# A selective scan in 1024-wide pieces: two scans a unit, with the carries added to the input, and the product with C shared anew between two engines

## The chip, the cores and the metric

One core of one Trainium2 chip. The metric is device time in microseconds (us) for one execution. Engines by their short names: PE is TensorE, DVE is VectorE, ACT is ScalarE, POOL is GpSimd, SP is SyncE. Every instruction stream is in order, and every dependency between engines is a semaphore written out by hand.

## The reference, cut to what matters

A Mamba block and then a mixture of experts, all in float32, on 8 sequences of 1024 tokens with 256 channels. The change is in the selective scan:

```
dA = exp(dt_t[:, :, None] * A[None])
dBu = (dt_t * u_t)[:, :, None] * B_t[:, None, :]
h = dA * h + dBu
y = einsum('bdn,bn->bd', h, C_t)
```

It has 512 inner channels, 16 states and 1024 time steps a sequence. `h` starts at zero in each of the 8 sequences. Before it lie a layer norm, an input projection, a convolution of four taps and the projections that give dt, B and C. After it come a gate, an output projection, a second norm, a router that picks 2 of 8 experts, and the expert products on tiles of 128 gathered tokens.

## The kernel before

The 8192 tokens are worked in 16 **blocks** `q` of T = 512 time steps. Two blocks make one sequence: an **even block** starts from a zero state, an **odd block** from the state that the even one left in `carry`. A block has UN = 16 **units** `n` (u = 16q + n). A unit is 128 inner channels (chunk c = n // 4) times 4 states (g = n % 4), laid out as 4 **segments** j. In each segment the 128 partitions hold 4 states of 32 channels, and the 512 time steps lie along the free dimension. Per unit:

- POOL `drive(u)` (L1326) multiplies the whole 128x2048 driving term `hs` = dt*u times B, one unit ahead. `hs` has three buffers, so it waits (through `s_ymm`) until PE has read unit u-3.
- ACT `decay(u, j)` (L977) writes exp(dt*A) of a segment into the PSUM tile `dA`, which has one buffer. Decays of the next unit are written when DVE has used the present one: segments 0 and 1 after the product L1123, segment 2 after L1136, segment 3 after its scan.
- DVE `scan` (L1114) runs one recurrence of 512 steps a segment, in the order 0, 1, 3, 2. It starts from 0.0 or from `carry[:, n, j]`. Segments 0 and 1 are multiplied by C in one 128x1024 product (L1123), segment 2 in a 128x512 product (L1136).
- POOL `weigh(u)` (L1334) multiplies segment 3 by C. The last column is left out in even blocks, since ACT still has to read the state there: `keep01`, `keep2` and `keep3` (L981, L985, L991, L994) copy the last states to `carry`, and `keep3` does that last product itself.
- PE `weigh` (L699) sums the states of a unit into `yps`.

The loops over `s` are **slots**: in slot s each engine works unit s, and between its parts of the unit whatever else is listed for the slot. That other work is the front of the next blocks, in the tables `MAKES` and `TAKES` (PE makes a result in the one PSUM bank `ring`, ACT takes it). It is also `round_off`, `less_lost`, `plus_relu`, `dtu` (four POOL steps of the softplus, by `pieces`), `deviation` (small POOL steps of the norms), `route`, `weights` and `place` (DVE, slots 6 and 8), the scatter of tokens (POOL, slots 8 to 11), and the expert tiles (`tile_transpose`, `gate_up`, `tanh`, `activate`, `down`, `take_y`, `add_rows`). SP issues the loads: `load_rep` brings dt and dt*u of a chunk, repeated for each of 4 states, from DRAM into `rep_dt` and `rep_dtu`, one chunk ahead. After unit 255 only expert tiles of the last block are left.

In DVE's slot, all that matters for the order is:

```
unit_first(s)      # scans 0 and 1, product L1123
unit_third(s)      # scan 3
weights, place     # slot 8 only
unit_second(s)     # scan 2
activate           # two 128x256 steps of an expert tile, in 8 of 16 slots
unit_last(s)       # product L1136
gated, route       # slots 0, 4, 8, 12 and slot 6
```

## Time and profile before

| | |
|---|---|
| median of 3 runs | 2355.94 us (2353.19 to 2358.41) |
| span of the profiled execution | 2343.2 us |
| DVE busy | 1891.2 us (81%) |
| POOL busy | 1961.7 us (84%) |
| ACT busy | 1808.0 us (77%) |
| PE busy, weight loads | 1793.1 us (77%), 922.2 us (39%) |
| mean granted TensorE clock | 0.884 |

The span is from the first to the last instruction of the one execution that was profiled. The profile gives no device time of its own for it, so 12.7 us lie between its span and the median. Times in rows are from the start of the span. From about 600 us to 1900 us the trace repeats with a period of two blocks, about 263 us. The stretch quoted below is one such period: block 8 (even) has its first scan at 1122.73 us, block 9 (odd) at 1255.4 us.

A busy share says how long an engine had an instruction in it. Neighbouring instructions of one engine can overlap in the trace by some 0.1 us, and on POOL by more: where the next one starts before the row's end, the distance between two starts is the better price.

### The profile page before, as it was taken

The numbers are of one execution on the slowest core, as the hardware profiler recorded it, in microseconds if no ns is written. First come the engines' busy times: TensorE is split into PE (matmuls) and PEld (weight loads), VectorE is DVE, ScalarE is ACT, GpSimd is POOL, SyncE is SP. The second block draws the span as 40 slices with busy tenths as digits, with TensorE's granted clock in tenths as the row PEclk, the third lists the DMA queues.
The fourth block names the chain that finished last, engine by engine and source line by source line (L and its number), as shares of the span: only waits on it lengthen the run. The fifth ranks groups of instructions, "written<-read, shape, count | busy, mean of one in ns | idle before, by whom it ended". The sixth has DMA issues, their size and how long they took to land.

```text
span 2343.2 us, 32677 instructions
## 1 busy us (share of the span) xinstructions
PE 1793.1 (77%) x7694; PEld 922.2 (39%) x7694; DVE 1891.2 (81%) x2437; ACT 1808.0 (77%) x3753; POOL 1961.7 (84%) x1320
## 2 busy tenths in 40 slices
PE   5666767597879778797878778697879788675785
PEld 2212323153435344353434344353435344343542
DVE  0399988898989988898979988898989989999221
ACT  5888878888888878888888878888888878763332
POOL 1588897989989898999989898989989898987333
PEclk9788878797989989898989999898989989786998
DMA  1545455477768777677768787677768787797332
GB/s 57 136 90 135 109 134 115 121 170 179 172 159 198 174 192 171 165 184 172 175 158 199 174 197 174 159 176 175 175 157 201 176 193 166 181 259 221 71 51 33
DMA packets 217980, 369.35 MB, mean 158 GB/s; under 512 B 31040, under 2 KB 86592, under 8 KB 217664
## 3 DMA queue, kind: packets, MB, share of 16 engines
q1 hardware_dynamic: 192208, 333.56, 58.0%
q0 software_dynamic: 25584, 33.71, 7.4%
q8 instruction: 65, 1.06, 0.2%
q14 instruction: 123, 1.01, 0.2%
HBM read 285.05 MB, written 83.01 MB: 157 GB/s over the span
## 4 chain that ended last, share of the span: by engine, by line
POOL 31%; issue 25%; PE 14%; ACT 12%; DVE 10%; DMA 7%; POOLq 1%; DVEq 0%; ACTq 0%; SPq 0%
POOL arena L1326 11%; DMA out<-yt,xt 6%; DVE dA L1114 5%; POOL arena L1334 5%; PE ring L605 4%; POOL sorted_x L1364 4%; POOL out L1374 3%; POOL rst L1290 3%; ACT dA L977 2%; DVE arena L1114 2%; POOL arena L1344 2%; POOL arena L1349 2%; PE yps L699 2%; PE ring L613 1%; PE ring L625 1%
## 5 line engine op out<-in xcount | busy, mean ns | idle before, releaser
L1326 POOL TENSOR_TENSOR arena<-arena,b_bc 128x2048 f32<-128x2048 f32 x256 | 998.6, 3901 | 64.8 <-PE yps L699 64.5
L977 ACT ACTIVATE dA<-arena,a_s 128x512 f32<-128x512 f32 x1024 | 680.7, 684 | 120.9 <-DVE arena L1123 74.7
L1114 DVE TENSOR_TENSOR_SCAN dA<-dA,arena 128x512 f32<-128x512 f32 x384 | 454.7, 1214 | 175.2 <-ACT dA L977 108.8
L1114 DVE TENSOR_TENSOR_SCAN dA<-dA,carry,arena 128x512 f32<-128x512 f32 x384 | 477.6, 1275 | 66.6 <-POOL arena L1326 49.8
L699 PE MATMUL yps<-arena,const_s 128*32 128x512 f32 x2048 | 321.3, 704 | 84.1 <-POOL arena L1334 53.6
L1334 POOL TENSOR_TENSOR arena<-arena,c_bc 128x511 f32<-128x511 f32 (+1 forms) x256 | 335.6, 1311 | 28.0 <-DVE arena L1114 26.4
L1123 DVE TENSOR_TENSOR arena<-dA,c_bc 128x1024 f32<-128x1024 f32 x256 | 313.6, 1225 | 8.8
L1374 POOL DMA_INDIRECT out<-yt,xt x135 | 214.7, 1590 | 116.5 <-ACT yt L1018 84.5
L597 PE MATMUL ring<-arena 128*128 128x512 f32 x488 | 271.7, 684 | 52.9 <-ACT arena L881 24.5
L731 PEld LDWEIGHTS p_g<-xT,w_e 128*128 128x128 f32 x1680 | 218.8, 211 | 125.4 <-issue 125.4
L605 PE MATMUL ring<-arena 128*128 128x512 f32 x480 | 235.3, 635 | 33.7 <-ACT arena L881 12.1
L731 PE MATMUL p_g<-xT,w_e 128*128 128x128 f32 x1680 | 238.8, 301 | 21.1 <-issue 12.0
L711 PE MATMUL p_a<-w_e,hT 128*128 128x256 f32 x420 | 128.2, 434 | 110.6 <-ACT xT L1010 81.4
L1136 DVE TENSOR_TENSOR arena<-dA,c_bc 128x512 f32<-128x512 f32 x256 | 176.4, 689 | 5.2
L1114 DVE TENSOR_TENSOR_SCAN arena<-dA,carry,arena 128x512 f32<-128x512 f32 x128 | 163.2, 1275 | 9.4 <-ACT dA L977 9.4
L1114 DVE TENSOR_TENSOR_SCAN arena<-dA,arena 128x512 f32<-128x512 f32 x128 | 155.3, 1213 | 18.4 <-ACT dA L977 18.4
L1364 POOL DMA_INDIRECT sorted_x<-xf,pos x128 | 127.5, 996 | 48.8 <-issue 33.5
L597 PEld LDWEIGHTS ring<-arena 128*128 128x128 f32 x488 | 93.5, 213 | 183.3 <-issue 91.7
L605 PEld LDWEIGHTS ring<-arena 128*128 128x128 f32 x480 | 90.7, 199 | 159.3 <-issue 94.8
L711 PEld LDWEIGHTS p_a<-w_e,hT 128*128 128x128 f32 x420 | 85.8, 215 | 158.7 <-issue 112.9
L699 PEld LDWEIGHTS yps<-arena,const_s 128*32 128x32 f32 x2048 | 43.5, 115 | 252.8 <-issue 166.1
L625 PE MATMUL ring<-w_out_s,sz 128*128 128x256 f32 x512 | 122.7, 382 | 4.5 <-ACT uc L885 3.6
(173 smaller groups left out, 2995.7 us busy)
## 6 DMA issues: line engine op xcount, KB each, us to landing
arena<-dt_d SPq DMA_DIRECT2D x512, 256.0 KB
w_e<-in_w_moe SPq DMA_DIRECT2D x105, 512.0 KB, 4.7
dt_d<-arena SPq DMA_DIRECT2D x128, 256.0 KB, 2.4
w_e<-in_w_moe SPq DMA_DIRECT2D x105, 256.0 KB
xt<-sorted_x SPq DMA_DIRECT2D x135, 129.0 KB
b_bc<-bc_d SPq DMA_DIRECT2D x256, 64.0 KB, 2.4
c_bc<-bc_d SPq DMA_DIRECT2D x256, 64.0 KB, 3.5
xs<-in_x SPq DMA_DIRECT2D x16, 512.0 KB, 4.4
```

The source lines that it names most:

```text
L597: last = pe.matmul(bank(q, name), w_in_s[:, c, ch * P:(ch + 1) * P], xnT[:, c, :], start=c == 0, stop=c == DC - 1)
L605: last = pe.matmul(bank(q, f"W{c}"), d_conv[:, c, k, :], ubuf[:, c % 2, k:k + T], start=k == 0, stop=k == TAPS - 1)
L699: last = pe.matmul(yps[32 * j:32 * j + 32, :], sumsel, hs[:, u % 3, j, :], start=False, stop=g == G - 1, skip_group_check=True)
L711: last = pe.matmul(p_a[:, DM:2 * DM], hT[:, v % 2, c, :], w_e[:, v % 2, col:col + DM], start=c == 0, stop=c == DC - 1)
L731: last = pe.matmul(p_g[:, f, :], w_e[:, v % 2, col:col + P], xT[:, v % 2, c, :], start=c == 0, stop=c == DC - 1)
L977: act.activation(dA[:, j, :], rep_dt[:, c % 2, j, :], ACT.Exp, scale=a_s[:, n, j:j + 1]).then_inc(s_exp, 1)
L1114: return dve.tensor_tensor_scan(out_ap, dA[:, j, :], hs[:, u % 3, j, :], init, ALU.mult, ALU.add)
L1123: dve.tensor_tensor(hs[:, u % 3, 0:2], dA[:, 0:2], c_bc[:, g, :].unsqueeze(1).to_broadcast([P, 2, T]), ALU.mult).then_inc(s_m01, 1)
L1326: pool.tensor_tensor(hs[:, u % 3], rep_dtu[:, c % 2], b_bc[:, g, :].unsqueeze(1).to_broadcast([P, J, T]), ALU.mult).then_inc(s_dbu, 1)
L1334: pool.tensor_tensor(hs[:, u % 3, 3, 0:end], hs[:, u % 3, 3, 0:end], c_bc[:, g, 0:end], ALU.mult).then_inc(s_hp, 1)
L1364: pool.indirect_dma_start(out=sorted_x, out_offset=bass.IndirectOffsetOnAxis(ap=pos[:, q % 2, k, t:t + 1], axis=0), in_=xf[:, q % 2, t, :] ...
L1374: pool.indirect_dma_start(out=out_rows, out_offset=bass.IndirectOffsetOnAxis(ap=number, axis=0), in_=yt[:, v % NY, :], in_offset=None, bou ...
```

## The change

Segments 0 and 1 are scanned in one 1024-wide recurrence, and segments 2 and 3 in another. What would run over from one segment into the next is cut off by a first decay of zero: column 0 of `rep_dt` is set once to 1e30 (`NEVER`), the loads leave that column alone (511 of 512 elements), and exp of a huge negative number is 0. The rates get an upper bound below zero for that (`SLOWEST`). So both scans start from 0.0, and in odd blocks the carry has to come in another way: carry times the true first decay is added to column 0 of the driving term. `load_first` fetches the true first dt (8-byte pieces into `dt0`, four DMAs a chunk of odd blocks), POOL `first_rates` multiplies by the rates, ACT `first_decay` takes the exp, POOL `first_carry` multiplies the carries, and DVE `add_carry(u)` adds 4 columns for unit u one slot ahead.

The product with C of segments 2 and 3 is 1024 wide too. In units 1, 4, 7, 10, 13 of a block (`POOLED`) it is POOL's, in place in `hs`, after the scan wrote there; in the other 11 DVE does it out of `dA`. POOL's `weigh` moves to the end of its slot. In even blocks it waits for ACT's `keep23`, which copies the last states first. ACT computes decays 2 and 3 one after the other at the end of the slot (before, 3 was in the middle).

```
-POOL: if 0 <= s < UN * NQ:
-          weigh(s)                      # ahead of deviation, less_lost ... dtu
+POOL: if 0 <= s < UN * NQ and pooled(s):
+          weigh(s)                      # last of the slot
+      for p, c in firsts(s + 2):
+          first_rates(p, c)
...
             def load_rep(q, c, part):
+                    skip = 1 if k == 0 else 0
-                        sp.dma_start(dst[32 * r:32 * r + 32, c % 2], src).then_inc(s[c % 2], 16)
+                        sp.dma_start(dst[32 * r:32 * r + 32, c % 2, :, skip:], src[:, :, skip:]).then_inc(s[c % 2], 16)
...
-            def keep2(u):
-            def keep3(u):
+            def keep23(u):
+                if pooled(u):
+                    act.wait_ge(s_h23, pooled_to(u))
+                    ends = hs[:, u % 3, 2:4, T - 1]
+                else:
+                    act.wait_ge(s_m23, kept_to(u))
+                    ends = dA[:, 2:4, T - 1]
+                act.activation(carry[:, u % UN, 2:4], ends, ACT.Copy).then_inc(s_carry23, 1)
...
+            def add_carry(u):
+                dve.wait_ge(s_dbu, u + 1)
+                dve.wait_ge(s_w0, CC * (q // 2) + n // G + 1)
+                dve.tensor_tensor(hs[:, u % 3, :, 0], hs[:, u % 3, :, 0], carry[:, n, :], ALU.add).then_inc(s_inject, 1)
+
+            def scan(u, j, out):
+                dve.wait_ge(s_exp, J * u + j + 2)
+                dve.wait_ge(s_dbu, u + 1)
+                if q % 2 == 1:
+                    dve.wait_ge(s_inject, UN * (q // 2) + n + 1)
+                return dve.tensor_tensor_scan(out.rearrange("p j t -> p (j t)"), dA[:, j:j + 2].rearrange("p j t -> p (j t)"),
+                                              hs[:, u % 3, j:j + 2].rearrange("p j t -> p (j t)"), 0.0, ALU.mult, ALU.add)
...
             def weigh(u):                # POOL
-                pool.wait_ge(s_h3, u + 1)
+                pool.wait_ge(s_h23, pooled_to(u))
+                if q % 2 == 0:
+                    pool.wait_ge(s_carry23, UN * (q // 2) + n + 1)
...
DVE slot:
                 if unit:
                     unit_first(s)
-                if unit:
-                    unit_third(s)
...
                 for g, k in tiles_in(s - 2):
                     activate(g, k)
-                if unit:
+                if (s + 1) // UN % 2 == 1 and 0 <= s + 1 < UN * NQ:
+                    add_carry(s + 1)
+                if unit and not pooled(s):
                     unit_last(s)
```

What DVE has in its stream in block 9 (odd) for units 11 and 12, before (scans print as SCALAR_TENSOR_TENSOR, L1123 and L1136 are the products with C):

```order
L1114 SCALAR_TENSOR_TENSOR dA<-dA,carry,arena 128x512 x2
L1123 TENSOR_TENSOR arena<-dA,c_bc 128x1024
L1114 SCALAR_TENSOR_TENSOR arena<-dA,carry,arena 128x512
L1114 SCALAR_TENSOR_TENSOR dA<-dA,carry,arena 128x512
L1136 TENSOR_TENSOR arena<-dA,c_bc 128x512
L1114 SCALAR_TENSOR_TENSOR dA<-dA,carry,arena 128x512 x2
L1123 TENSOR_TENSOR arena<-dA,c_bc 128x1024
```

And now the same place, unit 11 and the first two instructions of unit 12 (L1174 scan, L1181 product, L1165 the added carry):

```order
L1174 SCALAR_TENSOR_TENSOR dA<-dA,arena 128x1024
L1181 TENSOR_TENSOR arena<-dA,c_bc 128x1024
L1174 SCALAR_TENSOR_TENSOR dA<-dA,arena 128x1024
L1165 TENSOR_TENSOR arena<-arena,carry 128x4
L1181 TENSOR_TENSOR arena<-dA,c_bc 128x1024
L1174 SCALAR_TENSOR_TENSOR dA<-dA,arena 128x1024
L1181 TENSOR_TENSOR arena<-dA,c_bc 128x1024
```

Four scans became two, and the second product, now wider, stands behind `add_carry` of unit 12, which waits for `drive(12)`.

What POOL has in block 9 from `drive(8)` to `drive(9)`, before (L1326 drive, L1334 weigh, L1338 round_off):

```order
L1326 TENSOR_TENSOR arena<-arena,b_bc 128x2048
L1334 TENSOR_TENSOR arena<-arena,c_bc 128x512
L1338 TENSOR_TENSOR t_s<-t_s,arena 128x512
L1326 TENSOR_TENSOR arena<-arena,b_bc 128x2048
```

And now (L1389 drive, L1415 first_carry, L1419 round_off, L1398 weigh):

```order
L1389 TENSOR_TENSOR arena<-arena,b_bc 128x2048
L1415 TENSOR_TENSOR carry<-carry,e 128x16
L1419 TENSOR_TENSOR t_s<-t_s,arena 128x512
L1398 TENSOR_TENSOR arena<-arena,c_bc 128x1024
L1389 TENSOR_TENSOR arena<-arena,b_bc 128x2048
```

The product of unit 7 is twice as wide and stands directly ahead of `drive(9)`, behind `round_off`.

## Rows read from the trace of the kernel before

**Rows 1.** The page, busy time, share of the span and instructions of each engine.

```profile
PE 1793.1 (77%) x7694; PEld 922.2 (39%) x7694; DVE 1891.2 (81%) x2437; ACT 1808.0 (77%) x3753; POOL 1961.7 (84%) x1320
```

**Rows 2.** Who waited for whom: us in total, times, longest us.

```profile
DVE dA L1114 <- ACT dA L977: 114.3, 31, 83.9
...
DVE dA L1114 <- POOL arena L1326: 113.7, 53, 6.4
```

**Rows 3.** Groups by shape: count, busy us, mean ns, idle before and its releasers.

```profile
L1326 POOL TENSOR_TENSOR arena<-arena,b_bc 128x2048 f32<-128x2048 f32 x256 | 998.6, 3901 | 64.8 <-PE yps L699 64.5 <-issue 0.2
...
L994 ACT ACTIVATE arena<-carry,c_bc 128x1 f32<-128x1 f32 x128 | 37.7, 295 | 4.1
```

**Rows 4.** Timeline of DVE, unit 0 of block 8: start, us, instruction.

```profile
1122.73 2.34 DVE L1114 TENSOR_TENSOR_SCAN dA<-dA,arena 128x512 f32<-128x512 f32 x2
1125.11 1.22 DVE L1123 TENSOR_TENSOR arena<-dA,c_bc 128x1024 f32<-128x1024 f32 x1
1126.25 1.21 DVE L1114 TENSOR_TENSOR_SCAN arena<-dA,arena 128x512 f32<-128x512 f32 x1
1127.38 1.21 DVE L1114 TENSOR_TENSOR_SCAN dA<-dA,arena 128x512 f32<-128x512 f32 x1
1128.62 0.69 DVE L1136 TENSOR_TENSOR arena<-dA,c_bc 128x512 f32<-128x512 f32 x1
```

**Rows 5.** Timeline of DVE, block 9, units 2 and 3.

```profile
1276.34 1.27 DVE L1114 TENSOR_TENSOR_SCAN dA<-dA,carry,arena 128x512 f32<-128x512 f32 x1
...
1279.18 2.47 DVE L1114 TENSOR_TENSOR_SCAN dA<-dA,carry,arena 128x512 f32<-128x512 f32 x2 [0.84 <-POOL arena L1326]
```

**Rows 6.** Timeline of POOL ahead of `drive(3)` in block 9.

```profile
1272.61 1.67 POOL L1334 TENSOR_TENSOR arena<-arena,c_bc 128x512 f32<-128x512 f32 x1
1273.66 1.66 POOL L1338 TENSOR_TENSOR t_s<-t_s,arena 128x512 f32<-128x512 f32 x1
1274.71 4.38 POOL L1326 TENSOR_TENSOR arena<-arena,b_bc 128x2048 f32<-128x2048 f32 x1
```

**Rows 7.** Timeline of ACT: block 9, input of `round_off`; block 8, last decay of unit 6.

```profile
1272.47 0.63 ACT L910 ACTIVATE t_s<-t_s 128x512 f32<-128x512 f32 x1
...
1175.37 0.69 ACT L977 ACTIVATE dA<-arena,a_s 128x512 f32<-128x512 f32 x1
```

**Rows 8.** Timeline of DVE, block 8: scan 3 of units 6 and 7.

```profile
1175.11 1.22 DVE L1114 TENSOR_TENSOR_SCAN arena<-dA,arena 128x512 f32<-128x512 f32 x1 [3.37 <-ACT dA L977]
...
1183.56 1.21 DVE L1114 TENSOR_TENSOR_SCAN arena<-dA,arena 128x512 f32<-128x512 f32 x1
```

**Rows 9.** Timeline of POOL, block 8, from `weigh(7)` to the first scatter, and later.

```profile
1184.85 1.08 POOL L1334 TENSOR_TENSOR arena<-arena,c_bc 128x511 f32<-128x511 f32 x1
1185.88 1.09 POOL L1338 TENSOR_TENSOR t_s<-t_s,arena 128x512 f32<-128x512 f32 x1
1186.93 3.81 POOL L1326 TENSOR_TENSOR arena<-arena,b_bc 128x2048 f32<-128x2048 f32 x1
...
1193.11 1.02 POOL L1364 DMA_INDIRECT sorted_x<-xf,pos  x1 [0.61 <-DVE pos L1203]
...
1219.16 0.20 POOL L1308 TENSOR_TENSOR rst<-rst 128x4 f32<-128x4 f32 x1
```

**Rows 10.** Timeline of DVE: first scans of unit 12 in blocks 8, 9 and 10.

```profile
1225.46 2.35 DVE L1114 TENSOR_TENSOR_SCAN dA<-dA,arena 128x512 f32<-128x512 f32 x2 [5.71 <-POOL arena L1326]
...
1355.62 2.47 DVE L1114 TENSOR_TENSOR_SCAN dA<-dA,carry,arena 128x512 f32<-128x512 f32 x2 [5.70 <-POOL arena L1326]
...
1489.15 1.23 DVE L1114 TENSOR_TENSOR_SCAN dA<-dA,arena 128x512 f32<-128x512 f32 x1 [6.41 <-POOL arena L1326]
```

**Rows 11.** Timeline of ACT (`keep2(13)`) and POOL (`drive(15)`, `drive(16)`) in block 8.

```profile
1241.79 0.18 ACT L985 ACTIVATE carry<-dA 128x1 f32<-128x1 f32 x1
...
1241.92 4.38 POOL L1326 TENSOR_TENSOR arena<-arena,b_bc 128x2048 f32<-128x2048 f32 x1
...
1251.53 3.81 POOL L1326 TENSOR_TENSOR arena<-arena,b_bc 128x2048 f32<-128x2048 f32 x1
```

More of the change, by code:

```diff
@@ L45, with pooled, pooled_to, kept_to @@
 TAIL_AT = 9
+NEVER = 1.0e30
+SLOWEST = -1.0e-26
+POOLED = (1, 4, 7, 10, 13)
+def pooled(u):
+    return u % UN in POOLED
+def pooled_to(u):
+    return sum(pooled(v) for v in range(u + 1))
+def kept_to(u):
+    return u + 1 - pooled_to(u)
 class Batch:
@@ L136, in ahead, with firsts @@
     return [q for q in range(NQ) if s == (second if q == 1 else UN * (q - 2) + n)]
+def firsts(s):
+    return [(s // UN, s % UN // G)] if 0 <= s < UN * NQ and s // UN % 2 == 1 and s % G == 0 else []
 def made_in(s, place):
@@ L341, in mamba_moe @@
         s_carry01 = sem("s_carry01")
-        s_carry2 = sem("s_carry2")
+        s_carry23 = sem("s_carry23")
+        s_m23 = sem("s_m23")
+        s_h23 = sem("s_h23")
+        s_rate = sem("s_rate")
+        s_dt0 = [sem(f"s_dt0{i}") for i in range(2)]
+        s_first = sem("s_first")
+        s_e0 = sem("s_e0")
+        s_w0 = sem("s_w0")
+        s_inject = sem("s_inject")
         s_m01 = sem("s_m01")
-        s_m2 = sem("s_m2")
-        s_h3 = sem("s_h3")
-        s_carry3 = sem("s_carry3")
         s_hp = sem("s_hp")
@@ L471, in load_rep, with load_first @@
                     src = dt_d[q % 2, k, c].rearrange("(j d) t -> d j t", j=J)
+                    skip = 1 if k == 0 else 0
                     for r in part:
-                        sp.dma_start(dst[32 * r:32 * r + 32, c % 2], src).then_inc(s[c % 2], 16)
+                        sp.dma_start(dst[32 * r:32 * r + 32, c % 2, :, skip:], src[:, :, skip:]).then_inc(s[c % 2], 16)
+            def load_first(q, c):
+                sp.wait_ge(s_dtw[c % 2], 32 * (2 * q + c // 2 + 1))
+                wait(sp, s_first, CC * (q // 2) + c - 1)
+                src = dt_d[q % 2, 0, c].rearrange("(j d) t -> d j t", j=J)
+                for r in range(R):
+                    sp.dma_start(dt0[32 * r:32 * r + 32, c % 2], src[:, :, 0:2]).then_inc(s_dt0[c % 2], 16)
             def store_x2(q):
@@ L560, in _ @@
                     load_late((4, 5, 6, 7, 9, 10, 13, 14).index(n))
+                if 0 <= q < NQ and q % 2 == 1 and n in (0, 4, 8):
+                    load_first(q, n // G + 1)
+                if q >= 0 and front and q % 2 == 0 and n == 12:
+                    load_first(q + 1, 0)
                 if 0 <= q < NQ and n in (0, 4, 8):
@@ L1051, in _ @@
                     take_y(g, k)
+                for p, c in firsts(s + 1):
+                    first_decay(p, c)
                 if 0 <= s + 1 < UN * NQ:
@@ L1064, in _ @@
                         gap_exp(p)
-                if 0 <= s + 1 < UN * NQ:
-                    decay(s + 1, 3)
                 for g, k in tiles_in(s - 3, False):
@@ L1070, in _ @@
                     take(item)
-                if 0 <= s < UN * NQ and q % 2 == 0:
-                    keep2(s)
                 for item in taken_in(s, 4):
@@ L1076, in _ @@
                     take_xt(g, k)
+                if 0 <= s < UN * NQ and q % 2 == 0:
+                    keep23(s)
                 if 0 <= s + 1 < UN * NQ:
                     decay(s + 1, 2)
-                if 0 <= s < UN * NQ and q % 2 == 0:
-                    keep3(s)
+                    decay(s + 1, 3)
                 for g, k in tiles_in(s - 1):
@@ L1129, in unit_second, with unit_first @@
+            def unit_first(u):
+                scan(u, 0, dA[:, 0:2]).then_inc(s_scan, 1)
+                dve.wait_ge(s_scan, kept_to(u) + pooled_to(u) + kept_to(u - 1))
+                weigh(u, 0).then_inc(s_m01, 1)
             def unit_second(u):
-                scan(u, 2).then_inc(s_scan, 1)
+                if pooled(u):
+                    scan(u, 2, hs[:, u % 3, 2:4]).then_inc(s_h23, 1)
+                else:
+                    scan(u, 2, dA[:, 2:4]).then_inc(s_scan, 1)
             def unit_last(u):
-                q, n = u // UN, u % UN
@@ L1386, in _ @@
                     drive(s + 1)
+                for p, c in firsts(s + 1):
+                    first_carry(p, c)
                 for p in ahead(s, 9, -19):
@@ L1412, in _ @@
                     dtu(p, k)
+                if 0 <= s < UN * NQ and pooled(s):
+                    weigh(s)
+                for p, c in firsts(s + 2):
+                    first_rates(p, c)
 def program(nc, args):
```

111 lines of the change are left out of this document (58 added, 53 removed).

## The prediction

> **What bounds the kernel now.** I read the page first. POOL is busy for 84% of the span, DVE 81%, ACT and PE 77% each [rows 1]. No engine is idle enough for one busy share to set the time, so the waits come next. DVE's scans wait 113.7 us for POOL's driving term. They wait 114.3 us for ACT's decays, and the longest single wait there, 83.9 us, is the start of the program, so 30.4 us are left [rows 2]. The timeline then says where. In a period of two blocks DVE runs without a gap in most slots and stops in three places: up to 1 us in the slots around units 1 to 3, for `drive` (0.84 at unit 3 of block 9 [rows 5]); at unit 6, for a decay (3.37 [rows 8]); and at unit 12, 5.7 to 6.4 us for `drive(12)` [rows 10]. The last is the dearest: the scatters and the norm steps stand in POOL's slots 8 to 11, and POOL works through them from `drive(9)` on. So the bound changes hands: POOL in slots 8 to 11, DVE and POOL neck and neck in 12 to 3, ACT (fed by PE through one PSUM bank) and DVE in 4 to 7. The period, unit 12 of block 8 to unit 12 of block 10, is 1489.15 - 1225.46 = 263.7 us [rows 10]. I work the change out on it, block by block.
>
> **DVE's own work.** In an even block two scans back to back take 2.34, one alone 1.21, and a scan starts 1.13 after the one in front of it [rows 4]. So 0.08 of each instruction lies under the next, unless the next reads its result; then there is a gap of some 0.03 (1127.38 + 1.21 to 1128.62). A unit costs 1.13 + 1.25 + 1.14 + 1.13 + 1.24 + 0.61 = 6.50. The products give the fixed part: 1.22 for 1024 columns, 0.69 for 512, so 0.53 per 512 and 0.16 fixed [rows 4]. A scan with the same fixed part has 1.06 per 512, and a 1024-wide one costs 2.28. Its bounds are 2.12 (no fixed part) and 2.43 (two single ones); I take 2.28. New unit with the product on DVE: 2.31 + 1.14 + 2.31 + 1.15 = 6.91, so +0.41. New unit with it on POOL: 2.31 + 1.14 + 2.20 = 5.65, so -0.85. Eleven of the one and five of the other: +0.3 us an even block. In odd blocks a scan costs 1.27 and a pair 2.47 [rows 5], 0.06 more each, so a unit is 6.75 now. The new one is 6.91 plus some 0.05 for `add_carry` behind a scan (+0.21), or 5.65 plus 0.2 where scans 0 and 1 wait for its result (-0.9). That makes -2.2 an odd block. **So DVE gains about 2 us in 264**, not two fixed parts a unit: what the wide scan saves was mostly hidden already, and the wider product takes back the rest.
>
> The Trainium skill speaks for more. "VectorE: DVE Perf Modes", section "The DRAIN you can't avoid", says that the next operation does not start until the pipe is empty. By that rule each of 512 scans less would save its fixed part whole. The trace disagrees in size: starts 1.13 apart for a duration of 1.21 [rows 4].
>
> **POOL's own work.** A 512-wide product costs 1.05 from start to start (1184.85, 1185.88, 1186.93), `drive` with 2048 columns 3.81 [rows 9]. In between, 1024 columns cost 1.08 + 2.73/3 = 1.99; bounds are 1.9 (half of drive) and 2.1 (two of the small). 16 x 1.05 = 16.8 go and 5 x 1.99 = 10.0 come, -6.8 a block. Odd blocks get 8 small steps at 0.20 [rows 9], +1.6. This is a real gain only where POOL sets the pace.
>
> **ACT.** `keep3` goes in even blocks, some 0.42 a slot (two copies, the first like `keep2`'s 0.18 [rows 11], the second 0.295 [rows 3]). The decays keep their number, but decay 3 moves behind the slot's other work, so everything between comes 0.68 earlier and the second scan needs both decays.
>
> **Even block, walked through.** POOL at unit 1: the product now stands behind `round_off`, which waits for ACT, so `drive(3)` starts 0.7 later; the same order is priced for the odd block below. That is caught up by unit 6, where DVE waits for ACT anyway. There the last decay ends at 1176.06 [rows 7]. With five `keep3` and one decay's place less, it ends about 2.4 earlier, 1173.6. The wide scan and the product then take 2.31 + 1.15 from 1173.6, where now 2.34 + 0.61 follow 1175.11 [rows 8]: unit 7 starts 1.0 earlier. Unit 7 is POOL's. Its scan 3 ended at 1184.77 (1183.56 + 1.21 [rows 8]) and `drive(9)` started at 1186.93 behind two steps of 1.05 [rows 9]. Now the wide scan ends 1.07 later in the unit, and POOL waits for `keep23`, which ACT reaches at about 1185.5 by the same 2.4 and 0.7 earlier. 1185.6 + 1.99 = 1187.6 for `drive(9)`: **+0.7**. Slots 8 to 11 on POOL: the products of units 8 and 9 go (-2.1), that of unit 10 is 0.95 dearer, and of the 0.61 that the first scatter waits for DVE's positions [rows 9] all goes. -1.75 in all, so `drive(12)` and unit 12 come 1.0 earlier. Units 12 to 15: ACT reaches `keep2(13)` only at 1241.79, when POOL was just starting `drive(15)` at 1241.92 [rows 11]. `keep23(13)` comes at some 1240.2, the product ends at 1242.4, `drive(15)` is 0.5 later, and `drive` of the next block's unit 0 follows 9.61 behind it (1251.53 [rows 11]) less the product of unit 14, 1.05. It ends at 1254.8 where it was 1255.3. **Even block: -0.5.**
>
> **Odd block.** `round_off` of unit 1 gets its input from ACT at 1273.10 (1272.47 + 0.63 [rows 7]); decay 3's place makes that 1272.4. Then 1.05 for it and 1.99 for the product behind it: `drive(3)` starts at 1275.45 instead of 1274.71 [rows 6] and ends at 1279.25. DVE's order adds the rest. `add_carry(3)` waits for that drive, and unit 2's second product (1.15) is queued behind it, with unit 3's first scan behind both. 1279.25 + 0.15 + 1.2 = 1280.6 against 1279.18 [rows 5]: +1.4 at unit 3. Units 3, 5 and 6 cost +0.21 and unit 4 -0.9, and part of ACT's wait at unit 6 takes up the difference, but the second scan there now waits for both decays: still +1.4 at unit 7. Its product on POOL: scan +1.01 later in the unit (2.28 for 1.27), product +0.94, `round_off` no longer behind it -1.05: `drive(9)` +0.9, of which 0.15 was waited. **+2.15.** Slots 8 to 11 on POOL: -1.15 for products, -0.6 for the scatter's wait, +0.2 for `first_rates`. Then unit 12 has the same queue as unit 3: when `drive(12)` ends, `add_carry(12)` and unit 11's second product (1.35) come before the scan, which now starts at once [rows 10]. Sum -0.2. Units 12 to 15: 3 x 0.21 - 0.9 - 0.3 of a wait = -0.55. **Odd block: +1.4.**
>
> **Sum.** +0.9 us in two blocks. Of 16 blocks I count 7 pairs (the first two run before the expert tiles fill the slots): +6.5. The profiled execution has a span of 2343.2 and the median is 2355.9, so its 12.7 outside stay: 2349.7 + 12.7 = **2362 us**. I count nothing for the loads. 128 small DMAs join 1573 on SP's queue, and 256 of the large ones move 511 of 512 columns; chunks are fetched a chunk ahead. If that cover were gone, each of the 64 first units of a chunk would wait for its load.
>
> **Rivals.**
> 1. *POOL's relief comes through (0.27).* If the five products find POOL idle and `keep23` on time, the two queues behind `drive` shrink to nothing: slots 8 to 11 give -1.75 each block, the other terms about -0.5, -4 in a pair, -28: **2328**. For it: all waits for `drive`. Against: unit 7's product stands directly ahead of the costly slots.
> 2. *The scans save their fixed parts whole (0.10).* 512 x 0.16 = 82 less, 32 less for the pointer (0.06 x 512), 256 small products of 0.69 give way to 176 wide ones of 1.22 (+38), 128 carries at 0.20, as POOL's small step [rows 9] (+26). -50 on DVE: **2306**. This is the skill's rule from above. Against it are starts 1.13 apart.
> 3. *No visible change (0.15)*: DVE's gain and the added queues cancel, 2351 to 2361. Three runs of this kernel can't tell less than 0.2% from nothing.
> 4. *POOL's product is late in all five places (0.10).* In even blocks it needs `keep23`, at the end of ACT's slot, and `drive` two units on is queued behind it. At 1 us a place, 5 in a pair and 35 in all on top of the forecast: **2397**. It decides if ACT runs more than 1 us behind DVE at units 1, 4 and 10 as well. Late loads would cost about the same.
>
> The forecast, slightly slower, has 0.38. 2362 has its own range of 2360.7 to 2380. The whole range reaches down to rival 1, with 2.12 for a scan as its lower bound, and up to most of rival 4: **2325 to 2392**. Faster than 0.2%: 0.37 (1 and 2). Slower: 0.48 (forecast and 4).
>
> **What the new profile would show.** DVE scans at 2.28 and no gap between a product and the scan after it, so a free even unit of 6.9 or 5.65. POOL product near 2.0, and POOL's busy time about 95 us lower. In odd blocks unit 3 and unit 12: `add_carry` waiting for POOL, with the second product and the scan behind it. `drive(9)` directly behind unit 7's product. I am wrong if the wait at unit 12 shrinks by more than 2 us a block, if wide scans start closer together than the single ones did, or if the 511-column loads end a wait of ACT's decays.

## The result and the profile after

| | before | after |
|---|---|---|
| median (fastest to slowest) | 2354.57 us (2351.37 to 2358.41), 4 runs | 2595.43 us (2595.03 to 2600.82), 4 runs |
| ratio, 95% interval | 1 | 1.1035 (1.1006 to 1.1064) |
| span of the profiled execution | 2343.2 us | 2593.4 us |
| mean granted TensorE clock | 0.884 | 0.847 |

The change costs 241 us. I had forecast 2362, with 2325 to 2392 as the range: the sign was right and the size wrong by far. The page's line of busy times:

```profile
PE 1882.8 (73%) x7694; PEld 970.7 (37%) x7694; DVE 2053.1 (79%) x1974; ACT 1777.0 (69%) x3528; POOL 1863.4 (72%) x1209
```

Against [rows 1], POOL and ACT lost share, DVE gained busy time, and no engine is busier than 79%. So the time went into DVE instructions that I had not priced and into waits. The groups on DVE, and POOL's product (line, engine, operation, tiles, count | busy us, mean ns of one | idle before them and what ended it):

```profile
L1174 DVE TENSOR_TENSOR_SCAN dA<-dA,arena 128x1024 f32<-128x1024 f32 x432 | 989.6, 2291 | 230.3 <-ACT dA L1027 169.6 <-POOL arena L1389 57.7 <-issue 0.4
L1181 DVE TENSOR_TENSOR arena<-dA,c_bc 128x1024 f32<-128x1024 f32 x432 | 528.2, 1223 | 10.6
...
L1165 DVE TENSOR_TENSOR arena<-arena,carry 128x4 f32<-128x4 f32 x128 | 137.6, 1075 | 94.2 <-POOL carry L1415 60.3 <-POOL arena L1389 33.7
...
L1234 DVE TENSOR_SCALAR wv<-gap 128x4 f32<-128x4 f32 x16 | 39.7, 2481 | 0.2 <-ACT gap L1049 0.2
```

```profile
L1398 POOL TENSOR_TENSOR arena<-arena,c_bc 128x1024 f32<-128x1024 f32 x80 | 159.7, 1996 | 95.0 <-issue 49.6
```

The three big prices are as forecast: 2.29 for a wide scan (I took 2.28), 1.22 for a product, 2.00 for POOL's (1.99). What stands out is L1165, `add_carry`: four columns, 128 times, 1.075 us each. I had given it 0.05 to 0.2. Half of them do take 0.14 to 0.17; the other 63 take 127 us. The timeline of unit 13 in block 9, first DVE and then POOL (start, duration, ...), shows what a long one lies beside:

```profile
1512.26 0.42 DVE L1299 TENSOR_TENSOR hT<-th,p_g 128x256 f32<-128x256 f32 x1
1512.60 5.27 DVE L1165 TENSOR_TENSOR arena<-arena,carry 128x4 f32<-128x4 f32 x1
1517.79 1.21 DVE L1181 TENSOR_TENSOR arena<-dA,c_bc 128x1024 f32<-128x1024 f32 x1
```

```profile
1512.36 1.71 POOL L1419 TENSOR_TENSOR t_s<-t_s,arena 128x512 f32<-128x512 f32 x1
1513.41 4.42 POOL L1389 TENSOR_TENSOR arena<-arena,b_bc 128x2048 f32<-128x2048 f32 x1
```

There is no idle time before it, and it counts as busy for 5.27 us, where 65 others took 0.14 to 0.17. It ends at 1517.87 (1512.60 + 5.27), POOL's `drive` at 1517.83 (1513.41 + 4.42). All 63 long ones end within 0.1 us of the end of a POOL tensor_tensor. `weights` (L1234) is held in the same way, 2.5 us each, where it took 0.15 before. That is why the waits of the page do not show this loss.

Where the time went by blocks: from the first scan of a block's unit 0 to that of the next block, mean over the even blocks 4 to 12 and the odd blocks 3 to 11, with the part in which DVE ran nothing:

```
          even block  DVE idle   odd block  DVE idle
before       132.8      17.5       131.1      12.0
after        144.2      22.2       151.3      17.5
```

The period from unit 12 of block 8 to unit 12 of block 10 is now 295.8 (1651.93 - 1356.17), against 263.7 [rows 10]: +32.1 where I had +0.9.

```profile
1356.17 2.30 DVE L1174 TENSOR_TENSOR_SCAN dA<-dA,arena 128x1024 f32<-128x1024 f32 x1 [4.72 <-POOL arena L1389]
...
1651.93 2.30 DVE L1174 TENSOR_TENSOR_SCAN dA<-dA,arena 128x1024 f32<-128x1024 f32 x1 [4.95 <-POOL arena L1389]
```

In an odd block DVE is busy 14.7 longer and idle 5.5 longer; in an even one, which adds a carry only in its last slot, 6.8 and 4.6. So two things had to be explained: the holds, and a loss of some 11 us in a block that has almost no `add_carry`.

### The profile page after: what moved, and what is told of

It is laid out like the page before. It is cut to its first block, busy times and chain, and to the rows that moved or that the text cites. A ratio compares the mean times of both kernels' runs of the same rounds, so it can differ in the third digit from the quotient of the medians.

```text
span 2593.4 us, 31612 instructions
## 1 busy us (share of the span) xinstructions
PE 1882.8 (73%) x7694; PEld 970.7 (37%) x7694; DVE 2053.1 (79%) x1974; ACT 1777.0 (69%) x3528; POOL 1863.4 (72%) x1209
## 4 chain that ended last, share of the span: by engine, by line
DVE 24%; issue 22%; PE 19%; ACT 16%; POOL 15%; DMA 4%; POOLq 0%; ACTq 0%; DVEq 0%; SPq 0%
DVE dA L1174 12%; POOL arena L1389 8%; PE ring L649 6%; ACT dA L1027 4%; DMA out<-yt,xt 4%; DVE arena L1165 4%; DVE arena L1181 3%; PE yps L744 2%; PE ring L657 2%; PE p_g L776 2%; PE ring L641 2%; POOL rst L1353 2%; DVE wv L1234 2%; POOL out L1455 1%; PE ring L686 1%
## 5 line engine op out<-in xcount | busy, mean ns | idle before, releaser
L1174 DVE TENSOR_TENSOR_SCAN dA<-dA,arena 128x1024 f32<-128x1024 f32 x432 | 989.6, 2291 | 230.3 <-ACT dA L1027 169.6
L1389 POOL TENSOR_TENSOR arena<-arena,b_bc 128x2048 f32<-128x2048 f32 x256 | 983.2, 3841 | 110.9 <-PE yps L744 110.3
L1027 ACT ACTIVATE dA<-arena,a_s 128x512 f32<-128x512 f32 x1024 | 665.3, 682 | 234.5 <-DVE arena L1181 209.7
L1181 DVE TENSOR_TENSOR arena<-dA,c_bc 128x1024 f32<-128x1024 f32 x432 | 528.2, 1223 | 10.6
L744 PE MATMUL yps<-arena,const_s 128*32 128x512 f32 x2048 | 321.0, 702 | 114.6 <-POOL arena L1398 98.8
L641 PE MATMUL ring<-arena 128*128 128x512 f32 x488 | 298.0, 742 | 120.6 <-ACT sz L933 68.9
L649 PE MATMUL ring<-arena 128*128 128x512 f32 x480 | 251.1, 671 | 48.5 <-ACT arena L943 15.7
L1398 POOL TENSOR_TENSOR arena<-arena,c_bc 128x1024 f32<-128x1024 f32 x80 | 159.7, 1996 | 95.0 <-issue 49.6
L1165 DVE TENSOR_TENSOR arena<-arena,carry 128x4 f32<-128x4 f32 x128 | 137.6, 1075 | 94.2 <-POOL carry L1415 60.3
L641 PEld LDWEIGHTS ring<-arena 128*128 128x128 f32 x488 | 100.6, 229 | 256.1 <-issue 95.8
L1174 DVE TENSOR_TENSOR_SCAN arena<-dA,arena 128x1024 f32<-128x1024 f32 x80 | 182.3, 2279 | 0.0
L649 PEld LDWEIGHTS ring<-arena 128*128 128x128 f32 x480 | 98.3, 214 | 183.3 <-issue 104.9
L1419 POOL TENSOR_TENSOR t_s<-t_s,arena 128x512 f32<-128x512 f32 x64 | 77.0, 1204 | 102.5 <-ACT t_s L953 102.5
```

Source lines behind the costliest of these rows:

```text
L641: last = pe.matmul(bank(q, name), w_in_s[:, c, ch * P:(ch + 1) * P], xnT[:, c, :], start=c == 0, stop=c == DC - 1)
L649: last = pe.matmul(bank(q, f"W{c}"), d_conv[:, c, k, :], ubuf[:, c % 2, k:k + T], start=k == 0, stop=k == TAPS - 1)
L744: last = pe.matmul(yps[32 * j:32 * j + 32, :], sumsel, hs[:, u % 3, j, :], start=False, stop=g == G - 1, skip_group_check=True)
L1027: act.activation(dA[:, j, :], rep_dt[:, c % 2, j, :], ACT.Exp, scale=a_s[:, n, j:j + 1]).then_inc(s_exp, 1)
L1165: dve.tensor_tensor(hs[:, u % 3, :, 0], hs[:, u % 3, :, 0], carry[:, n, :], ALU.add).then_inc(s_inject, 1)
L1174: return dve.tensor_tensor_scan(out.rearrange("p j t -> p (j t)"), dA[:, j:j + 2].rearrange("p j t -> p (j t)"), hs[:, u % 3, j:j + 2].rea ...
```

## Experiments

**Theory 1**: a small DVE instruction with two operands in SBUF is held until POOL's running instruction ends. **Theory 2**: it is the new order of decays and products. **Theory 3**: the chain that makes a carry (rates on POOL, exponential on ACT, product on POOL) is waited for. Theories 4 and 5 came later. All times are medians; before ran at 2356 to 2357 beside each of them.

### The hold by itself, in the kernel before

```
                 dve.wait_ge(s_scan, 2 * u + 2)
+                if (u + 1) // UN % 2 == 1:
+                    dve.tensor_tensor(spare[:], a_s[:, n, :], a_s[:, n, :], ALU.add)   # small_sbuf
+                    dve.tensor_tensor(spare[:], dA[:, 2, 0:J], a_s[:, n, :], ALU.add)  # small_psum
+                    dve.tensor_scalar(spare[:], a_s[:, n, :], 1.0, None, ALU.mult)     # small_single
```

Each kernel has one of the three lines.

> The kernel before with one more DVE instruction in each of 128 slots (those whose next unit is in an odd block), ahead of the product of segment 2: four columns, both operands in SBUF, into a spare tile that nobody reads; nothing waits for it. Theory 1: it is held until POOL's instruction ends. POOL is busy 84% of the time with instructions of 1 to 3.8 us, so a hold of some 1 us on the average and 128 x 1 = 128 more on DVE, of which a part falls into its idle time: 2400 to 2480. Theory 2: it costs its own 0.15, 128 x 0.15 = 19: 2355 to 2376.

> The same additional instruction at the same place, with the first operand from PSUM instead of SBUF. Theory 1: no hold, as the products of segment 0 and 1 (one operand in PSUM) show none: each is 0.15 to 0.2 long, 2355 to 2378 in all. Were it held like the one with two operands in SBUF, what holds it is not the pair of operands in SBUF, and both runs give the same time.

> The kernel before with 128 small DVE instructions as in the run with two operands in SBUF (which took 1.94 each and 2545 in all), but each a tensor_scalar with a single operand in SBUF, output in SBUF. The weights' tensor_scalar took 2.1 to 3.5 in the changed kernel, so theory 1 in its wider form (float32 tensor_scalar from SBUF to SBUF is held as well) gives 2500 to 2560 and a mean above 1.5. In its narrow form (only two operands in SBUF are held): 0.15 each, 2355 to 2376.

Measured, in this order: 2545.29 (ratio to the kernel before 1.0824, 95% interval 1.0786 to 1.0862), **2363.53** (1.0038, 1.0022 to 1.0053) and 2541.71 (1.0794, 1.0760 to 1.0829). The groups of the added instruction, in this order:

```profile
L1138 DVE TENSOR_TENSOR spare<-a_s 128x4 f32<-128x4 f32 x128 | 248.0, 1938 | 2.5
```
```profile
L1138 DVE TENSOR_TENSOR spare<-dA,a_s 128x4 f32<-128x4 f32 x128 | 20.4, 159 | 2.5
```
```profile
L1138 DVE TENSOR_SCALAR spare<-a_s 128x4 f32<-128x4 f32 x128 | 252.1, 1970 | 2.5
```

The first two kernels differ in one operand's memory and by 182 us. With an operand in PSUM none of 128 is longer than 0.17, though 85 of them start while a POOL tensor_tensor runs. With both in SBUF 115 are long, and all of them end with a POOL tensor_tensor. The third shows that it isn't the number of operands: one operand and the result in SBUF, as `weights` has, is held as well. I had expected 1 us a hold and up to 2480 from both in SBUF; it was 1.94 us on the average and 2545. One reason is that a hold is not always over with the instruction that POOL is running. One that outlasted two more, in the kernel with both in SBUF:

```profile
1140.68 4.98 DVE L1138 TENSOR_TENSOR spare<-a_s 128x4 f32<-128x4 f32 x1
```
```profile
1139.72 1.11 POOL L1337 TENSOR_TENSOR arena<-arena,c_bc 128x512 f32<-128x512 f32 x1
1140.77 1.11 POOL L1347 TENSOR_TENSOR arena<-arena,t_s 128x512 f32<-128x512 f32 x1
1141.81 3.82 POOL L1329 TENSOR_TENSOR arena<-arena,b_bc 128x2048 f32<-128x2048 f32 x1
```

POOL's three follow each other without a gap, and DVE comes in at 1145.6, behind the last. That is not the rule: of the 115 long ones, 28 ran past at least one place where the next POOL tensor_tensor follows without a gap (142 of the 248 us), and 45 ended at such a place. What decides between the two is not shown. The Trainium skill, "SBUF — State Buffer", sections "SBUF: two separate sides" and "Who interferes with whom", says that DVE and GpSimd share one pair of ports under an exclusive lock that is held for the whole instruction, and that a DVE instruction with at most one SBUF input outside the 2-port modes does not contend. The twins agree (159 ns against 1938). The third kernel has one SBUF input and was held all the same, so by that rule its tensor_scalar would have to run in a 2-port mode; no row here shows the mode. Going by the Trainium skill I would have priced the hold in these rows as the rest of one POOL instruction; it lasted over the rest of one and two more.

### The carries off DVE, and out

```
-                dve.tensor_tensor(hs[:, u % 3, :, 0], hs[:, u % 3, :, 0], carry[:, n, :], ALU.add).then_inc(s_inject, 1)
+                pool.tensor_tensor(hs[:, u % 3, :, 0], hs[:, u % 3, :, 0], carry[:, n, :], ALU.add).then_inc(s_inject, 1)
...
                 for p, c in firsts(s + 1):
                     first_carry(p, c)
+                if (s + 1) // UN % 2 == 1 and 0 <= s + 1 < UN * NQ:
+                    add_carry(s + 1)
```

> The changed kernel with the carry added on POOL, right behind the drive of its unit, instead of on DVE; all else as it is. Theory 1 (a DVE instruction of four columns with two operands in SBUF is held until POOL's running instruction ends): the 137.6 us of the 128 additions on DVE leave it, of which some 117 are over the 0.15 to 0.17 that one takes when POOL is idle; POOL gets 128 x 0.2 = 26. 2595 - 117 + at most 26, so 2460 to 2500. Theory 2 (the time was lost to the new order of ACT's decays and POOL's products, and the long additions only fill time that would be waited anyway): 2575 to 2600.

> The changed kernel without the addition of carries, and without the three small steps that prepare it (rates on POOL, exponential on ACT, product on POOL); the blocks of odd number then start from zero, so this part of the computation is left out. The small loads stay. Theory 1: 2595 - 137 = 2458, and 0 to 15 below the run with the addition on POOL. Theory 3 (the chain POOL, ACT, POOL, DVE that makes a carry is itself waited for, at the first unit of each group of four): clearly below that, 30 us or more under the run with the addition on POOL. Theory 2: 2570 or more.

Measured: **2469.07** (1.0479, 1.0441 to 1.0516) with the addition on POOL and 2425.00 (1.0303, 1.0271 to 1.0335) without it. Moving one small instruction to another engine gives back 126 of the 241 us, as theory 1 says; an odd block falls from 151.3 to 138.8. Without any carry it is 44 less again, which is what theory 3 had asked for (30 or more). But this run also frees POOL of 128 x 0.2 = 26, and how the 44 divide is not shown; a run below tries the chain by itself. The loss of 69 that remains is there without any carry being added. In it the router's small instructions (`weights`, and the one-hot of `route`) stand out, held as well:

```profile
L1209 DVE TENSOR_TENSOR hot<-ix,const_s 128x64 f32<-128x64 uint32 x16 | 48.1, 3009 | 0.6
L1223 DVE TENSOR_SCALAR wv<-gap 128x4 f32<-128x4 f32 x16 | 41.4, 2585 | 0.2 <-ACT gap L1049 0.2
```

### The router's steps off DVE, and the rates early

The one-hot (DVE's `is_equal` of index and column number) becomes a difference on POOL and 1 minus its square, cut at zero, on ACT:

```
-                then(dve.tensor_scalar(wv[:, 0], e, 1.0, 2.0, ALU.add, ALU.mult))
...
-                then(dve.tensor_tensor(wv[:, 1], w0, e, ALU.mult))
...
-                dve.tensor_tensor(gap[:, :, 0], mx[:, :, 1], mx[:, :, 0], ALU.subtract).then_inc(s_gap, 1)
...
+                act.activation(wv[:, 0], gap[:, :, 1], ACT.Identity, scale=2.0, bias=two[:]).then_inc(s_ge, 1)
...
+                act.activation(xf[:, q % 2, :, DM], xf[:, q % 2, :, DM], ACT.Identity, scale=-1.0, bias=half[:]).then_inc(s_swap, 1)
...
+                pool.tensor_tensor(gap[:, :, 0], mx[:, :, 1], mx[:, :, 0], ALU.subtract).then_inc(s_gap, 1)
...
+                pool.tensor_tensor(hot[:], ixf[:].unsqueeze(3).to_broadcast([P, 2, QT, NE]),
+                                   iota.unsqueeze(1).unsqueeze(1).to_broadcast([P, 2, QT, NE]), ALU.subtract).then_inc(s_hd, 1)
...
+                act.activation(hot[:], hot[:], ACT.Square).then_inc(s_hd, 1)
...
+                act.activation(hot[:], hot[:], ACT.Relu, scale=-1.0, bias=1.0).then_inc(s_hot, 1)
```

> The run with the addition on POOL, and besides the router's small DVE instructions with two operands in SBUF (or one, for the weight's tensor_scalar) moved off DVE: the difference of the two best logits and a subtraction for the one-hot to POOL, square, relu and the weights' linear steps to ACT; DVE keeps the maxima and one reciprocal. Theory 1: in the run with the addition on POOL those 48 instructions took 84.2 us (42.8, 31.0 and 10.4) where they take 0.14 to 0.23, some 9 us, when POOL is idle. 2469 - 75, plus up to 20 for the two steps on POOL and five on ACT a block: 2394 to 2420. Theory 2 (order of decays and products): 2455 to 2480.

> The same move in the run without the addition of carries (its odd blocks start from zero, which is left out of the computation as there). What is left is the change without any DVE instruction that can be held. Theory 1: 2425 - 97 + 9, plus up to 20: 2337 to 2360, so not slower than the kernel before by more than 0.2%. Theory 2: 2410 to 2430.

> The kernel before with the router's steps moved in the same way: what the move itself costs where hardly anything is held. Those instructions take 7.5 us (the difference, 4.9 over its usual 0.17), 3.6 and 2.4 there. Theory 1: 0 to 20 us slower, 2353 to 2376. If it gains more than 10 us, the router's steps cost DVE more than their durations show and the gain of the other runs is not all from holds.

> The run with the addition and the router's steps off DVE, and the rates for a group's carries made on POOL directly behind the drive of the slot instead of at its end. Theory 3 (the chain of rates, exponential and product is waited for): ACT waited 45.1 us in 8 places for the rates in the run with the addition on POOL, 5.6 each; 20 to 45 us less than the run without this edit. Without theory 3: within 8 us of it.

(In that run the call of `first_rates` stands directly behind that of `first_carry` in POOL's slot.)

Measured, in this order: 2445.38 (1.0393, 1.0339 to 1.0448), 2404.20 (1.0201, 1.0158 to 1.0244), 2367.36 (1.0044, 1.0019 to 1.0070) and 2441.81 (1.0365, 1.0321 to 1.0409). **Both first expectations were missed**: 24 and 21 came back, not 75 and 88. With `weights` gone DVE stands at the next step, the first of `place`. It needs ranks that PE and ACT make from the one-hot, and my move makes that one later. And it has two operands in SBUF as well, so I was wrong to expect that nothing was left that can be held. In the run without carries it took 3.6 us in all, with 3.2 of idle time before it. Without carries and with the move:

```profile
L1256 DVE TENSOR_TENSOR row<-hot,r 128x64 f32<-128x64 f32 x16 | 17.9, 1120 | 33.4 <-issue 29.9 <-ACT r L1014 3.5
```

That is 30 us more idle and 14 more held. In the kernel before, the move brings 23.5 us of idle time to this step (5.9 to 29.4) and costs 10 us. So these runs do not price the router's holds by themselves: the move takes 75 to 88 us of holds away and brings some 45 us of waiting and new holds. Making the rates early is worth 4 us, within what the runs can tell apart, although ACT's 45 us of waiting at the exponential are gone with it. So this first link of theory 3's chain was on no path that counts.

### POOL's products

In the runs with no addition on DVE the even blocks were still at 138 to 142. DVE waits there in the slot of unit 2, and in the changed kernel's block 9 POOL shows why:

```profile
1410.74 1.08 POOL L1419 TENSOR_TENSOR t_s<-t_s,arena 128x512 f32<-128x512 f32 x1 [3.31 <-ACT t_s L953]
1411.79 1.99 POOL L1398 TENSOR_TENSOR arena<-arena,c_bc 128x1024 f32<-128x1024 f32 x1
1413.74 3.80 POOL L1389 TENSOR_TENSOR arena<-arena,b_bc 128x2048 f32<-128x2048 f32 x1
```

The rounding step waits 3.31 for ACT, and product and drive of unit 3 are queued behind it. **Theory 4**: that place is the loss. **Theory 5**: the products on POOL are, wherever they stand. Three runs start from the one with the rates early, and one from the changed kernel. `product_first` moves the call of `weigh` ahead of `round_off` in POOL's slot; `product_later` makes it `weigh(s - 1)`, directly behind `drive(s + 1)`. The other two are

```
-POOLED = (1, 4, 7, 10, 13)
+POOLED = ()
```

> The run with the rates made early, and POOL's product of segments 2 and 3 issued ahead of the slot's rounding step (which waits for ACT) instead of behind it. Theory 4 (what is left of the loss lies in the slot of unit 2, where DVE idles some 3.0 a block against 1.0 before, since the product and the drive of unit 3 stand behind that rounding step): 15 x 1.5 to 2 less, 2442 - 30 = 2405 to 2420. If the drive is then only waited for by an ACT that is itself late, less than 8 us.

> The run with the rates made early, and POOL's product of a unit issued in the next slot, behind the drive of the unit after that, so it delays no drive that DVE is to need first. If the loss from the products is the delayed drive: 2442 less 30 to 60, 2382 to 2412. If it is that PE gets the product late (PE waited 96 to 106 us for it) and with it its clock and all that is queued on PE: 2435 to 2480.

> The run with the rates made early, with all 16 products of segments 2 and 3 on DVE and none on POOL. DVE gets 5 x 1.14 = 5.7 a block, POOL loses 5 x 1.99 = 10.0. If POOL sets the pace of the slots that wait (theory 4, and the waits in the slots of units 10 and 11): 0 to 5 less a block, 2360 to 2440. If DVE does, in all slots: 16 x 5.7 = 91 more, 2533; I expect 2440 to 2500, since DVE idles some 18 a block.

> The changed kernel with one edit: all 16 products of segments 2 and 3 on DVE, none on POOL; the carries are added on DVE as there. Theory 5 (POOL's product of 2 us, issued between one drive and the next and behind a rounding step that waits for ACT, delays drives and PE): as in the runs with the addition on POOL, where the same edit gave 64 less, so 2595 - 64 = 2531, 2505 to 2550, with the additions' holds still there. If the products on POOL only hurt together with the additions on POOL: 2590 or more, up to 2595 + 91.

Measured, in this order: 2448.93 (1.0411, 1.0376 to 1.0446), 2440.12 (1.0361, 1.0340 to 1.0382), **2377.48** (1.0102, 1.0070 to 1.0134) and **2512.71** (1.0672, 1.0649 to 1.0695). Theory 4 falls: the slot of unit 2 got 1.1 shorter in odd blocks, and others longer. The product behind the next drive gives nothing either, as my second range had it (2435 to 2480): DVE waits less for drives, but PE twice as long for its input. The waits of the run with the rates early and of that one:

```profile
PE yps L749 <- POOL arena L1406: 103.1, 20, 13.3
...
DVE dA L1187 <- POOL arena L1397: 58.0, 35, 4.9
```
```profile
PE yps L749 <- POOL arena L1406: 211.6, 52, 17.0
...
DVE dA L1187 <- POOL arena L1397: 24.9, 16, 2.9
```

Taking the products away helps at any rate: 64 us there, and 83 in the changed kernel itself, although DVE gets 80 more instructions of 1.22 (98 us). I had thought 2440 to 2500 likelier for the first of these two.

In the changed kernel the even block falls from 144.2 to 132.1, just under the 132.8 of before. The odd one stays at 151.0 against 151.3, with the additions still held (144.3 us in all): there the products show nothing until the additions are off DVE, and then taking them away gives 4.0 (136.7 to 132.7). So the two causes account for most of the loss: the additions' holds in the odd blocks, POOL's products in the even ones, and in the odd ones once the holds are gone. The two are not independent. Without the products on POOL the router's small steps meet fewer of its instructions, and most of their holds go too. `weights` in the changed kernel with all products on DVE:

```profile
L1234 DVE TENSOR_SCALAR wv<-gap 128x4 f32<-128x4 f32 x16 | 4.3, 267 | 0.2 <-ACT gap L1049 0.2
```

It took 39.7 us with the products on POOL, and `route`'s one-hot 13.6 where it is now 3.6. So up to 45 of the 83 us can be holds of this kind. In the same way the step of `place` falls from 23.3 to 3.6 us between the run with the rates early and `all_on_dve`.

Of theory 2 this leaves the order of ACT's decays, which no run changes by itself. Without the start of the program DVE waited 58 us for decays before, 116 in the changed kernel and 64 in the one with all products on DVE. That kernel has the new order too, and its even blocks are no longer than before; so the order alone costs little there.

### What is left, and what the wide scan is worth

`pooled_4` is `all_on_dve` with `POOLED = (4,)`; `pooled_4_plain` the same with the router's steps on DVE; `all_dve_plain` has them on DVE and `POOLED = ()`. `narrow_scans` is `all_on_dve` with

```
-                return dve.tensor_tensor_scan(out.rearrange("p j t -> p (j t)"), dA[:, j:j + 2].rearrange("p j t -> p (j t)"),
-                                              hs[:, u % 3, j:j + 2].rearrange("p j t -> p (j t)"), 0.0, ALU.mult, ALU.add)
+                dve.tensor_tensor_scan(out[:, 0], dA[:, j], hs[:, u % 3, j], 0.0, ALU.mult, ALU.add)
+                return dve.tensor_tensor_scan(out[:, 1], dA[:, j + 1], hs[:, u % 3, j + 1], 0.0, ALU.mult, ALU.add)
```

> The run with all products on DVE (2377), but the product of unit 4 on POOL as in the changed kernel. Slots 3 to 6 took 32.0 with five products on POOL and 35.1 with none in even blocks, 24.2 against 25.1 for slots 4 to 6 in odd ones, while slots 1 to 3, 7 to 8 and 10 to 15 were longer with them: 8 x 3.1 + 8 x 0.9 = 32 less, 2345 to 2377. If any product on POOL costs more than it saves: 2380 or more.

> The same, with the router's small instructions left on DVE as in the changed kernel. Moving them cost 10 in the kernel before and gained 24 in the changed one with the addition on POOL; with only one product on POOL, and so fewer drives met, I expect between the two: 2350 to 2395, within 15 of the run with them moved. If they are held as in the changed kernel: 20 to 30 above it.

> The changed kernel with three edits: carries added on POOL, the rates made early, all products on DVE; the router's small instructions stay on DVE as before. With all products on DVE an even block took 132.1 in the run that still adds carries on DVE, 134.9 with the router's steps moved; the odd ones 132.7 with them moved. If leaving them is right: 2377 - 8 x 2.8 = 2355, up to 2377. If POOL's more crowded odd blocks hold them: 2377 to 2400.

> The run with all products on DVE and the router's steps moved (2377), with each scan of 1024 columns issued as two of 512, both from zero; results and all else are the same, so this run prices the wide scan itself. By starts 1.13 apart, two scans ahead of the instruction that needs them cost 2.36 where the wide one costs 2.32: 512 x 0.04 to 0.06, 20 to 31 more, 2397 to 2408 if DVE sets the pace everywhere, 2377 to 2397 where it idles. If each instruction less saves its whole fixed part of 0.16: 82 more, 2459.

Measured, in this order: 2384.09 (1.0118, 1.0095 to 1.0141), 2399.19 (1.0188, 1.0167 to 1.0209), 2396.41 (1.0188, 1.0151 to 1.0224) and 2410.93 (1.0247, 1.0218 to 1.0275). One product on POOL, in the place that I had picked by my sum of slots, gains nothing that these runs can show, where I expected up to 32 us (the ratios' intervals, 1.0095 to 1.0141 and 1.0070 to 1.0134 without it, overlap). The router's steps are better off DVE by 15 to 19 here. No version comes below the kernel before; the nearest, 2377, is 1% above it. The wide scans themselves do pay: 33 by the medians (3 more than the most I expected), and 20 by the blocks (134.9 + 135.2 against 132.7 + 134.9, times 8). The blocks are read from the fastest of six executions with narrow scans, 2394.56, so the two numbers need not agree. The groups of the two narrow scans, and of the wide one:

```profile
L1187 DVE TENSOR_TENSOR_SCAN dA<-dA,arena 128x512 f32<-128x512 f32 x512 | 626.6, 1224 | 176.9 <-ACT dA L1032 130.2 <-POOL arena L1414 29.0 <-POOL arena L1397 16.4
L1188 DVE TENSOR_TENSOR_SCAN dA<-dA,arena 128x512 f32<-128x512 f32 x512 | 617.3, 1206 | 0.0
```
```profile
L1187 DVE TENSOR_TENSOR_SCAN dA<-dA,arena 128x1024 f32<-128x1024 f32 x512 | 1172.7, 2290 | 183.8 <-ACT dA L1032 134.8 <-POOL arena L1414 30.8 <-POOL arena L1397 17.3
```

By durations alone the wide scans would save 71 (626.6 + 617.3 - 1172.7); part of it was no cost before, since each instruction lies under the next by some 0.08.

## Why the prediction failed, step by step

- **Scan, product, POOL's product** were priced right: 2.29, 1.22 and 2.00 measured. "DVE gains about 2 us in 264" holds for the work itself: scans and products of two blocks (unit 12 of block 8 to that of block 10) occupy DVE 207.2 us now and 209.4 before (each instruction up to the start of the next), -2.2. Rival 2, whole fixed parts saved, is out: 20 to 33 us for 512 scans less, where 82 was its term. The Trainium skill, "VectorE: DVE Perf Modes", section "The DRAIN you can't avoid", which I had read as speaking for that rival, says besides that a next operation that is not held starts earlier. The starts 1.13 apart agree with that.
- **The step that failed** is "6.91 plus some 0.05 for `add_carry` behind a scan", and in rival 2 "128 carries at 0.20". I took the price from a small step on POOL [rows 9] and looked only at how long such an instruction takes by itself. It measured 1.075 on the average, 5.54 at worst. Moved to POOL it gives back 126 us, more than half of the loss, and the twins in the kernel before show the cause: with both operands in SBUF it is held while POOL's instruction runs. The profile of before had two hints that I did not take up: `route`'s first difference took 470 ns on the average for four columns, and another small instruction of that size 148.

```profile
L1156 DVE TENSOR_TENSOR gap<-mx 128x4 f32<-128x4 f32 x16 | 7.5, 470 | 0.5
...
L1174 DVE TENSOR_SCALAR wv<-gap 128x4 f32<-128x4 f32 x16 | 2.4, 148 | 0.2 <-ACT gap L998 0.2
```

- **Even block, "-0.5"**: +11.4 measured. My walk followed POOL's queue through units 1, 7 and 8 to 11, and counted the products at units 8 and 9 as time given back. It had unit 7 1.0 earlier in the block than before and unit 12 as well; they came 3.7 and 7.1 later. With all products on DVE the block is at 132.1, so it is the five on POOL that cost it, with the router's holds that come with them. That products on POOL cost time is **rival 4**, which I had priced at 5 us in a pair and given one chance in ten: it measured 64 to 83 us in all, 7 to 12 in a pair of these blocks. Its mechanism, a drive queued behind a late product, is not shown: behind the drive, the product cost as much. PE waited 98.8 us for POOL's product in 20 places, up to 14.1, where it had waited 53.6 before, and that wait was nowhere in my sum.
- **Odd block, "+1.4"**: +20.2 measured. The queue at unit 3 is there as described: `add_carry` waits 3.13 for the drive, with the product and unit 3's scan behind it.

```profile
1417.58 1.04 DVE L1165 TENSOR_TENSOR arena<-arena,carry 128x4 f32<-128x4 f32 x1 [3.13 <-POOL arena L1389]
1418.54 1.21 DVE L1181 TENSOR_TENSOR arena<-dA,c_bc 128x1024 f32<-128x1024 f32 x1
1419.68 2.28 DVE L1174 TENSOR_TENSOR_SCAN dA<-dA,arena 128x1024 f32<-128x1024 f32 x1
```

  But unit 3 comes 4.2 later in its block than before (28.0 against 23.8), not 1.4. In block 9 the addition's hold is 0.9 of it. The larger part is ACT's input to the rounding step, which I had 0.7 earlier than before: counted from the block's first scan it comes at 19.3, where it was 17.7.
- **Rival 1**, POOL's relief, did not come: POOL is relieved (1863 us busy), and the time that it gains is idle. **Rival 3**, no visible change, is out as well.
- **The loads**, counted at nothing: in the profile after no load ends a wait of ACT's decays. This was not tried by itself, but the even blocks of 132.1 have them too.
- **The chain of rates, exponential and product**, which my sum left out, showed 60 us of waits at `add_carry` and 40 at ACT's exponential. With its rates made early the time fell by 4 us; the product at its end was not tried by itself.
- **Small slips in the working**: DVE's 30.4 us of waits for decays leave out 27.8 at the scan of segment 3, and seven pairs at +0.9 are +6.3, not +6.5. Neither changes the forecast's outcome.

What stays open: how the products' 64 to 83 us divide between late drives, a late PE, the router's holds and PE's clock. Both places that I tried on POOL left the time where it was. And the edits of the second half were made on kernels that already had the first ones, so the shares (126, 24, 4, 64) are those of this order of edits.

## What to carry to other kernels

Before a small DVE instruction is added, look at where its operands lie and what POOL does at that time. Two operands in SBUF, or a float32 tensor_scalar from SBUF to SBUF, cost the rest of the instruction that POOL was running, here at times that of the next ones too, and the profile books it as DVE's busy time: compare the mean duration of a small group with its minimum. With one operand in PSUM a small step took 0.16, and the additions on the engine that had held them up took 0.2. And a product moved to an engine that has room is not free: here 98 us more on DVE made the kernel 83 us faster.

## What the hardware showed that I had not expected

- A held DVE instruction is sometimes not let in between two POOL instructions that follow each other without a gap: 4.98 us over three, 5.27 over two, up to 7.03. In the changed kernel 28 of the 63 long additions did end at such a place, so this is no rule.
- A fall of PE's clock can follow a wait for another engine. In block 9 PE stood idle for 1.99 us, waiting for ACT, and of the 20 matmuls of the output projection behind it the first ten or so ran at half clock. Windows of that stretch (length, busy time and count of PE, PEld, DVE, ACT, POOL, then the granted clock, where 0.50 is 1.2 GHz, the DMA share and GB/s):

```profile
1396.00:1399.00 3.00, 1.07 (x10) 0.88 (x8) 3.00 (x5) 2.97 (x5) 0.67 (x1) 1.00 1.08 225
1399.00:1400.00 1.00, 0.94 (x4) 0.82 (x5) 1.00 (x1) 0.98 (x2) 0.92 (x2) 0.79 1.10 254
1400.00:1403.00 3.00, 3.00 (x9) 2.38 (x8) 2.97 (x3) 2.56 (x5) 2.92 (x3) 0.50 1.09 260
1403.00:1406.00 3.00, 2.31 (x11) 1.70 (x9) 2.52 (x4) 1.48 (x6) 2.85 (x2) 1.00 0.99 345
```

  ACT waits for those matmuls (1.52 us at 1405.35), and its input to the rounding step of unit 2 comes behind them. An estimate from the mean clocks puts PE at half clock for 544 us of the span before (2 x 0.116 x 2343.2) and 794 after. That this is a cause, and not only a consequence, of the lost time was not tried.
